# Layernorm tiles three to five transposed in 32x32 blocks by VectorE and moved by DMA, with weights loaded in pieces of 1024 columns

## What is computed

```python
def _layernorm(x, axis=-1, eps=1e-5):
    m = jnp.mean(x, axis=axis, keepdims=True)
    v = jnp.var(x, axis=axis, keepdims=True)
    return (x - m) / jnp.sqrt(v + eps)
# attention in blocks of 64 tokens, 8 heads of 128
q, k, v = (src @ W + b).reshape(B, nb, 64, 8, 128)
probs = softmax(einsum('bnqhd,bnkhd->bhnqk', q, k) * 128 ** -0.5)
out = einsum('bhnqk,bnkhd->bnqhd', probs, v).reshape(B, S, D) @ Wo + bo
# feed-forward, then a count of spikes over 5 steps of the same y
h = square(relu(x @ W_fc.T)); y = h @ W_proj.T
x = x + attn(_layernorm(x)); x = x + spikes(y(_layernorm(x))) / 5
```

## Time and profile before

| | us |
|---|---|
| median of 3 runs | 723.45 (723.35 to 725.72) |
| profiled execution, its own time | 722.57 |
| span of its slowest core | 721.0 (the eight cores: 719.0 to 721.0) |
| TensorE busy | 708.1 |
| VectorE busy | 383.3 |
| ScalarE busy | 184.4 |

### The profile page before, as it was taken

How to read it: one execution, slowest core, us unless ns; L and a number is a source line. 1 busy time by engine, 2 the same in 40 slices (tenths; PEclk the granted TensorE clock), 3 DMA queues, 4 the chain that set the end, 5 groups by cost and what they waited for, 6 DMA issues and landing times.

```text
span 721.0 us, 10986 instructions; the slowest of 8 cores (719.0 to 721.0 us)
## 1 busy us (share of the span) xinstructions
PE 708.1 (98%) x3892; PEld 332.4 (46%) x3892; DVE 383.3 (53%) x657; ACT 184.4 (26%) x342; POOL 26.1 (4%) x53
## 2 busy tenths in 40 slices
PE   7999999999999999999999999999999999999996
PEld 3544444454454444444444444444444444444444
DVE  5325646666575666524785224775225676221476
ACT  3553350461164034121002331001332001332000
POOL 2210000000001000000000000000000000000000
PEclk8999999999999999999999999999999999999999
DMA  8996863175248998697155000145100142100011
GB/s 173 203 161 152 147 138 125 73 173 148 118 104 204 180 210 199 160 221 157 60 123 168 30 1 23 65 123 165 34 1 12 77 127 78 59 1 1 30 45 44
DMA packets 21221, 77.80 MB, mean 108 GB/s; under 512 B 2864, under 2 KB 3120, under 8 KB 18736
## 3 DMA queue, kind: packets, MB, share of 16 engines
q0 software_dynamic: 6768, 31.46, 24.0%
q1 hardware_dynamic: 11952, 37.23, 16.9%
q10 hardware_dynamic: 2448, 8.40, 2.9%
HBM read 82.33 MB, written 16.78 MB: 137 GB/s over the span
## 4 chain that ended last, share of the span: by engine, by line
PE 93%; DMA 5%; DVE 1%; issue 1%; POOL 0%; DVEq 0%; POOLq 0%
PE ps_m L392 31%; PE ps_y L461 30%; PE ps_m L339 13%; PE ps_m L365 8%; PE ps_m L379 8%; DMA wq_sb<-Wq 4%; PE ps_y L414 1%; PE ps_y L442 1%; DMA xr<-x 1%; DVE acc_sb L703 1%; PE ps_t L321 1%; PE ps_t L426 0%; DVE acc_sb L700 0%; POOL wq_sb L789 0%; DVE xr L708 0%
## 5 line engine op out<-in xcount | busy, mean ns | idle before, releaser
L392 PE MATMUL ps_m<-xn2t,w_sb 128*128 128x512 bf16 x1024 | 224.5, 379 | 0.0
L461 PE MATMUL ps_y<-w_sb,h_sb 128*128 128x512 bf16 (+1 forms) x1024 | 218.3, 376 | 0.0
L461 PEld LDWEIGHTS ps_y<-w_sb,h_sb 128*128 128x128 bf16 x1024 | 100.2, 98 | 117.6
L392 PEld LDWEIGHTS ps_m<-xn2t,w_sb 128*128 128x128 bf16 x1024 | 98.9, 98 | 116.9
L543 ACT ACTIVATE h_sb<-ps_m 128x512 bf16<-128x512 f32 x128 | 76.4, 597 | 259.8 <-PE ps_m L392 259.8
L693 DVE TENSOR_TENSOR h_sb<-h_sb 128x512 bf16<-128x512 bf16 x128 | 53.4, 424 | 120.7 <-ACT h_sb L543 120.7
L703 DVE SCALAR_TENSOR_TENSOR acc_sb<-ps_y,acc_sb 128x1024 bf16<-128x1024 f32 (+2 forms) x72 | 78.6, 1092 | 7.9 <-DVE acc_sb L703 0.5
L339 PE MATMUL ps_m<-xnt,wk_sb 128*128 128x512 bf16 x248 | 58.6, 379 | 0.0
L365 PE MATMUL ps_m<-wv_sb,xnt 128*128 128x512 bf16 x256 | 58.3, 380 | 0.0
L339 PE MATMUL ps_m<-xnt,wq_sb 128*128 128x512 bf16 x240 | 56.9, 380 | 1.2 <-DMA wq_sb<-Wq 1.2
L379 PE MATMUL ps_m<-wo_sb,attn_sb 128*128 128x512 bf16 x256 | 55.9, 379 | 0.0
(11 more groups left out here) (62 smaller groups left out, 378.5 us busy)
## 6 DMA issues: line engine op xcount, KB each, us to landing
xr<-x SPq DMA_DIRECT2D x32, 512.0 KB, 10.1
xl<-x SPq DMA_DIRECT2D x24, 512.0 KB
w_sb<-Wfc POOLq DMA_DIRECT2D x8, 1024.0 KB, 14.5
x<-xr ACTq DMA_DIRECT2D x16, 512.0 KB, 4.1
w_sb<-Wpr POOLq DMA_DIRECT2D x8, 1024.0 KB, 33.9
out<-xr POOLq DMA_DIRECT2D x12, 512.0 KB, 3.3
xn2t<-blk SPq DMA_DIRECT2D x48, 64.0 KB, 2.0
wq_sb<-Wq POOLq DMA_DIRECT2D x8, 256.0 KB, 8.3
```

The source lines that it names most:

```text
L392: m = E.matmul(bank(key)[:], w1_sb[fc // 4][:, k0:k0 + 128], tokens(xn2t, c, 0, 4), start=(c == 0), stop=(c == 7))
L461: return E.matmul(out, h_sb[fc][:, tt * 128:(tt + 1) * 128], w2_sb[fc // 4][:, k0:k0 + n], start=(fc == 0), stop=(fc == 31))
```

## The change

Units 8 to 19 now take the way that units 20 to 31 took. The eight transposes on TensorE and the copy on ScalarE of each of them are gone; VectorE does `ln_blocks` one s after `ln_scale` instead (in blocks 0 to 2, behind the softmax work of that s), and SyncE does `turn_tile` for tiles three, four and five at the end of its part of a block. Three places are used for the blocks in turn, each free at that time: one inside the region of the first input rows, one in xnt[0] and the old one. The loads of xl for all units from 8 on fetch the 32-row stripes that the block layout wants, and those of tile five wait for all four stored parts of x2, not one. The semaphore of the block DMAs is split in two. Wo and each eighth of Wfc and Wpr are loaded by several DMAs of 1024 columns, 8 and 4 of them, on one semaphore, and the waits count them all.

```diff
 def ln_turn(b, s):
-    return ln_unit(b, s, 3 if b == -1 else 4)
+    return ln_unit(b, s, 3) if b == -1 else None
-BY_DMA = 20
+BY_DMA = 8
...
-    blk = at("blk", WORK + 57344, 4096, BF16)
+    blk = [at("blk_0", W1A + 32768, 4096, BF16), at("blk_1", WORK, 4096, BF16),
+           at("blk_2", WORK + 57344, 4096, BF16)]
...
     def tile_turned(n):
-        if 4 * n < BY_DMA:
+        if n < 2:
             return turned_copied(4 * n + 3)
-        return ld_turn, 256 * (n + 1 - BY_DMA // 4)
+        return ld_turn[n % 2], 256 * (n // 2)
+
+    def blocks_of(n):
+        return blk[0 if n < 4 else 1 if n == 4 else 2]
...
                 if p == 0:
-                    E.wait_ge(ld_wo, 16)
+                    E.wait_ge(ld_wo, 16 * 8)
...
-                E.wait_ge(ld_w1[fc // 4], 16)
+                E.wait_ge(ld_w1[fc // 4], 16 * 4)
...
-                    E.wait_ge(ld_w2[fc // 4], 16)
+                    E.wait_ge(ld_w2[fc // 4], 16 * 4)
...
                             ALU.subtract, ALU.mult).then_inc(ve_xn, 1)
-            if i >= BY_DMA:
-                ln_blocks(i)
         def ln_blocks(i):
             n, u = divmod(i, 4)
-            if u == 0 and i > BY_DMA:
+            if u == 0 and n in (3, 6, 7):
                 E.wait_ge(*tile_turned(n - 1))
             E.wait_ge(ve_xn, i + 1)
-            dst = blk[:].rearrange("p (a c u t) -> p c a u t", a=4, c=8, u=4)
+            dst = blocks_of(n)[:].rearrange("p (a c u t) -> p c a u t", a=4, c=8, u=4)
...
                 if (i := ln_unit(b, s, LN_SCALE)) is not None:
                     ln_scale(i)
+                if b >= 0 and (i := ln_unit(b, s, LN_BLOCKS)) is not None:
+                    ln_blocks(i)
...
+        def w_pieces(dst, src, done):
+
+            for j in range(src.shape[1] // 1024):
+                w_load(dst[:, j * 1024:(j + 1) * 1024], src[:, j * 1024:(j + 1) * 1024], done)
+
         def w1_load(i):
-            w_load(w1_sb[i][:], w1_h[i], ld_w1[i])
+            w_pieces(w1_sb[i], w1_h[i], ld_w1[i])
         def w2_load(i):
-            w_load(w2_sb[i][:], w2_h[i], ld_w2[i])
+            w_pieces(w2_sb[i], w2_h[i], ld_w2[i])
...
-        w_load(wo_sb[:], wo_h, ld_wo)
+        w_pieces(wo_sb, wo_h, ld_wo)
...
-            if i < BY_DMA:
-                if n >= 4:
-                    E.wait_ge(st_x2[u], 16 * (n - 3))
-                src = rows(src, u)
-            else:
+            if n >= 4:
                 for tt in range(4):
                     E.wait_ge(st_x2[tt], 16 * (n - 3))
-                src = src.rearrange("(i u t) d -> u i t d", i=4, u=4)[u]
-            E.dma_start(out=xl[i % 2][:], in_=src).then_inc(ld_xl[i % 2], 16)
+            E.dma_start(out=xl[i % 2][:],
+                        in_=src.rearrange("(i u t) d -> u i t d", i=4, u=4)[u]).then_inc(ld_xl[i % 2], 16)
...
         def turn_tile(n):
             E.wait_ge(ve_blk, 4 * n + 4 - BY_DMA)
-            E.wait_ge(*filled(("up", n - 5, 31)))
+            if n < 4:
+                E.wait_ge(*filled(("v", n - 2, 3, 1)))
+            elif n > 4:
+                E.wait_ge(*filled(("up", n - 5, 31)))
             dst = ln_tile(n)
             for i in range(4):
                 for a in range(4):
                     E.dma_start(out=dst[32 * a:32 * a + 32, i * 1024:(i + 1) * 1024],
-                                in_=blk[32 * i:32 * i + 32, a * 1024:(a + 1) * 1024]).then_inc(ld_turn, 16)
+                                in_=blocks_of(n)[32 * i:32 * i + 32, a * 1024:(a + 1) * 1024]
+                                ).then_inc(ld_turn[n % 2], 16)
...
             for i in (4 * b + 12, 4 * b + 13):
                 xl_load(i)
+            turn_tile(b + 2)
```

More of the change, by code:

```diff
@@ L106, in main_order @@
     return {k: n for n, k in enumerate(keys)}
-LN_STATS, LN_RSTD, LN_SCALE = 0, 1, 2
+LN_STATS, LN_RSTD, LN_SCALE, LN_BLOCKS = 0, 1, 2, 3
 def ln_unit(b, s, step):
@@ L246, in build_nc @@
     ve_blk = sem("ve_blk")
-    ld_turn = sem("ld_turn")
+    ld_turn = [sem(f"ld_turn{i}") for i in range(2)]
     full_s, free_s = sem("full_s"), sem("free_s")
@@ L765, in vector_program @@
                 ln_stats(i + 1)
-                ln_scale(i)
-                ln_scale(i + 1)
+                for j in (i, i + 1):
+                    ln_scale(j)
+                    ln_blocks(j)
                 ln_stats(i + 2)
@@ L770, in vector_program @@
                 ln_scale(i + 2)
+                ln_blocks(i + 2)
                 ln_stats(i + 3)
                 ln_scale(i + 3)
+                ln_blocks(i + 3)
             else:
```

## The result

| | before | after |
|---|---|---|
| median of 4 runs each, us | 724.59 | 756.13 (755.09 to 759.21) |
| ratio, 95% interval | | 1.0438 (1.0394 to 1.0482) |
| profiled execution, spans of the cores | 719.0 to 721.0 | 741.8 to 754.8 |
| TensorE busy on the slowest core | 708.1 | 709.0 |
| VectorE busy on the slowest core | 383.3 | 394.8 |

What follows compares the result with a forecast made beforehand. TensorE was taken as the bound; twelve removed `turn_x` at 0.45 us gain 5.4 us, added VectorE and DMA work costs 0, so 723.45 - 5.4 = 718.05 us, range 716.9 to 722.3.

Steps and rivals of the forecast that it cites:

- The bound: Whole kernel: TensorE, busy 708.1 of 721.0 us; only its work or its waits can change the time.
- The gain of 5.4 us: TensorE stream: removing `turn_x` from twelve units saves 0.45 us each, 5.4 us, all on the path.
- 275 ns a transpose: TensorE: skill page's figure, 26.4 us for 96 transposes; the sum used the trace's 0.056 us each instead.
- rival (c): Blocks 1 and 2: VectorE, 7.58 of 8.30 us busy, becomes the bound; 3 us, 721; chance 0.08.
- rival (b): First q group of block 1: tile three late by 16 serial issues, 2 to 5 us, 720 to 723; chance 0.10.
- the prediction's list of signs: Sign of being right: tile three's last block DMA issued at about 122, some 3 us ahead of the q group.
- 8 of an xl load ahead: SyncE's queue, tile five: 32 block packets an engine plus 8 of an xl load, 40 turns in all.
- The step on what stands behind something on a queue: SyncE's queue: xl and xr loads stand behind `turn_tile`, and nobody waits for them.
- rival (e): First up group: tile five late by 9 us, 727, up to 731 with stores of x2; chance 0.07.
- the term 40 x 0.88 = 35 us: Tile five beside large weight packets: 40 x (0.74 + 0.14) = 35 us, from 226.6 to 262, 9 us too late.
- rival (d): Down matmuls: last eighth of Wpr, cover about 2 us, comes late; about 2 us, 720; chance 0.07.

Runs made afterwards that it cites:

- e8_split_xr_late: Changed kernel, all xl loads in four DMAs, first feed-forward tile's four xr loads issued behind xl loads of units 22 and 23: 719.08 us, ratio 0.9933.
- e1_split: Changed kernel with each xl load issued as four DMAs of one 32-row stripe: 723.3 us, ratio 1.0002 against the kernel before.
- e2_stripes_only: Kernel before with only the xl loads of units 8 to 19 changed to the striped source: 737.74 us, ratio 1.0214.
- e10_split_20_21: Changed kernel with only the xl loads of units 20 and 21 in four DMAs each, all others striped: 737.71 us, ratio 1.0201.
- e7_split_to_19: Changed kernel with xl loads in four DMAs for units 8 to 19 only, the others striped: 737.09 us, ratio 1.0179.
- e6_split_no_pieces: Changed kernel with xl loads in four DMAs and Wo, Wfc and Wpr in whole DMAs: 753.66 us, ratio 1.0408.
- e3_pieces_only: Kernel before with only Wo, Wfc and Wpr loaded in pieces of 1024 columns: 723.35 us, ratio 1.0007.

## Why the prediction was wrong, point by point

**The bound** was read rightly: of the 33.8 us lost all but 0.8 are waits of TensorE, or its half clock behind them, less the gain.

**The gain of 5.4 us** was right. In e8_split_xr_late, core 6, a k and the next q group without `turn_x` start 2.04 us apart, the number taken from the earlier trace rows, and four groups of block 1 take 8.30 us, as worked out, instead of 8.75:

```profile
84.90 1.89 PE L343 MATMUL ps_m<-xnt,wk_sb 128*128 128x512 bf16 x8
...
86.94 1.90 PE L343 MATMUL ps_m<-xnt,wq_sb 128*128 128x512 bf16 x8
...
139.27 1.90 PE L343 MATMUL ps_m<-xnt,wq_sb 128*128 128x512 bf16 x8
...
147.57 1.90 PE L343 MATMUL ps_m<-xnt,wq_sb 128*128 128x512 bf16 x8
```

The 275 ns a transpose of the page of the Trainium skill that the prediction quotes were no guide here; the 0.056 us of the trace were.

**VectorE, rival (c)**, was costed rightly at nothing once its data came in time: 7.11 of 8.30 us busy in such a stretch of e8_split_xr_late (worked out: 7.58), and a wait of TensorE for probabilities of 0.4 us in all. (The 24 block transposes take 29.8 us instead of 14.9 for twelve, as worked out; the page's busy time of VectorE rose by 11.5 and not by 15.) The stall of the kernel after has rival (c)'s mark, a wait of L430 for p_sb, but not its cause: VectorE wasn't overloaded, it waited for a DMA.

**Tile three, rival (b)**, was right too. In e1_split the last block transpose ends at 108.2, the 16 issues follow, and the q group starts 4.2 us behind the last issue (the times worked out give 127.0 - 122.4 = 4.6, though the prediction's list of signs says "some 3"):

```profile
106.96 1.24 DVE L643 STREAM_TRANSPOSE blk<-xn 128x1024 bf16<-128x1024 bf16 x1
108.33 11.74 SPq L896 DMA_DIRECT2D xnt<-blk  x16
124.29 0.76 PEld L343 LDWEIGHTS ps_m<-xnt,wq_sb 128*128 128x128 bf16 x5
```

**The step that failed** is the cost of the xl loads. The change has three parts for units 8 to 19: the transposes, the block DMAs and the stripes in which their rows are loaded. I put the third in the description and costed it at nothing without naming what would hide it. The loads appear in the working only as "8 of an xl load ahead", eight packets an engine, which is a load on all 16 engines; 128 rows on four engines are 32 packets on each. It is same bytes, same 4 KB rows and same issue, but a quarter of the engines. The page "DMA: Bandwidth & Descriptors" of the Trainium skill had the rule (cited above), and the trace had the row at 25.5% and VectorE's 7.6 us at unit 22. The price, by the runs that kept one part of it: with the two stalls of VectorE alone 14.8 us over the kernel before (e2_stripes_only; e10_split_20_21 gives 14.9, though it has the transposes' gain), with tile five's 18.5 us of waiting alone 13.3 us over it, that gain included (e7_split_to_19). The step on what stands behind something on a queue was wrong for the same reason: I asked who waits behind `turn_tile`, not what stands ahead of it on the same engines.

**Tile five, rival (e)**, named the right place, tile and sign, and the wrong price and condition. I had 9 us if the pieces failed; they didn't fail, and 18.2 us came from the two striped loads ahead. Without pieces it is 31.5 us even with spread loads, so the term 40 x 0.88 = 35 us was far too small. What was mis-sized is the number of turns. The kernel before, 361 to 374 us, where the earlier trace rows count 769 packets of tile six's block DMAs:

```profile
DMA packets 914, 1.59 MB, mean 123 GB/s; under 512 B 272, under 2 KB 272, under 8 KB 913
```

Sixteen DMAs of 64 KB are 512 rows of 2 KB; the other 257 are small packets, one for each DMA on each engine (16 x 16 = 256). So a tile is 48 packets an engine and not 32, and a load in four DMAs is 8 + 4. The small ones take a turn like the others. In e6_split_no_pieces, core 5, 250 to 270 us, while tile five's blocks are under way:

```profile
q0 software_dynamic: 355, 2.63, 79.5%
q10 hardware_dynamic: 355, 1.26, 15.9%
q1 hardware_dynamic: 353, 0.49, 7.8%
```

The three queues take strict turns, and q1's packets average 1.4 KB. A round takes 20 x 16 / 355 = 0.90 us here, with the stores of x2 (q10), which the 35 us didn't have either. An estimate: from 226.6 to 242 us q1 moved 295 packets, 18.4 an engine; the other 41.6 of 60 take 41.6 x 0.90 = 37.5 us, until 279.5, and TensorE resumed at 281.6. So the turns were the right mechanism, and the count was wrong.

**The last eighth of Wpr, rival (d)**, was real with its cover of about 2 us: in e1_split it is 2 to 4 us late and eats the gain. I had it at 7%, as an alternative to the gain; it comes with it. Open is why e3_pieces_only, with the same pieces and the same 30.5 us between the first issue and the need (309.7 to 340.2, and 302.9 to 333.4 in e1_split), has no such wait.

## What to carry to other kernels

Before moving a load to another access pattern, work out on how many DMA engines it runs: look for a stretch where it is alone and read its queue's share (a quarter means 4 of 16), and split it by its outermost dimension if that is small. A DMA on few engines delays everything behind it on its queue by those engines, also transfers that use all 16. Count the small packet that ends each DMA on each engine, too: beside large packets of another queue it costs a full round, so many small DMAs are dear there. When a part of a change has "same bytes, same rows" as its whole cost, it still needs a row of its own.

## What was not expected of the hardware

The number of engines follows the outermost size so strictly that one load cut in two became slower (12.9% of 16 engines, 832 us), while the same load cut in four became faster (723 us). Weight loads cut into pieces of 1024 columns keep their rate and yet change who else gets through: 31.5 us for a tile of blocks, and 2 to 4 us the other way for Wpr. The packet that ends a DMA is a few bytes and still costs a whole round of the queues (355, 355 and 353 packets in 20 us). And a stall can cost more than itself: behind waits of 18.2, 6.0 and 5.4 us, and behind one of 4.4 us in e1_split, TensorE came back at the lower clock of 1.2 GHz (granted 0.50), and each time lost another 2.1 to 2.4 us.
